# Group normalisation before a two-way scan: the fourth channel tile's scale made in one batch of four samples instead of three and one

## The reference, cut to what matters

```python
def step(prev, x_i):
    y = jnp.einsum('oc,nch->noh', Wc, prev) + conv_b[None, :, None]
    y = jnp.where(y >= 0, y, prelu_a * y)
    cur = y + x_i
    return (cur, cur)
# v = group norm of x (32 groups of 16 channels, over the group's channels, H and W)
_, fwd_rest = jax.lax.scan(step, x[0], x[1:])                  # over W, forwards
_, bwd_rest = jax.lax.scan(step, fl[-1], fl[:-1], reverse=True)  # and back
x = x + conv(group_norm(x))
```

## Time and profile before

| | |
|---|---|
| median of 3 runs | 378.11 us (378.09 to 378.15) |
| the profiled execution | 378.27 us, of which the span that the trace shows is 376.5 us |
| PE busy | 352.3 us, 94% of the span |
| DVE / ACT / POOL busy | 286.5 / 226.7 / 19.3 us |
| head: last x piece read to PE's first k = 3 unit | about 4 us, at 34.9 to 38.7 us |

### The profile page before, as it was taken

One profiled execution on the slowest core, in us unless ns is written; L12 is line 12 of the kernel. 1 busy time (PEld: TensorE's weight loads), 2 busy tenths in 40 slices (PEclk: granted clock), 3 DMA queues, 4 the chain that ended last, 5 costly groups with the idle time before them and its releaser, 6 DMA issues.

```text
span 376.5 us, 10089 instructions
## 1 busy us (share of the span) xinstructions
PE 352.3 (94%) x3102; PEld 350.7 (93%) x3102; DVE 286.5 (76%) x925; ACT 226.7 (60%) x798; POOL 19.3 (5%) x30
## 2 busy tenths in 40 slices
PE   0169999999999999999999999999999999999996
PEld 0169999999999999999999999999999999999996
DVE  2678897888888888656656778778787787787786
ACT  3764566566565565665655656656656556566564
POOL 2177100000000000000000000000000000000000
PEclk9999999999999999999999999999999999999999
DMA  8998000000000000000000112212212112122122
GB/s 313 419 415 303 3 0 0 1 0 0 1 0 0 0 1 0 0 0 0 0 0 0 58 61 78 84 56 84 84 56 84 73 66 84 58 81 84 56 111 84
DMA packets 10664, 26.30 MB, mean 70 GB/s; under 512 B 1312, under 2 KB 1568, under 8 KB 10656
## 3 DMA queue, kind: packets, MB, share of 16 engines
q1 hardware_dynamic: 10512, 26.22, 18.0%
q10 hardware_dynamic: 144, 0.00, 0.0%
HBM read 13.63 MB, written 12.58 MB: 70 GB/s over the span
## 4 chain that ended last, share of the span: by engine, by line
PE 90%; DMA 5%; SPq 2%; ACT 1%; DVE 1%; issue 1%; POOL 0%; DVEq 0%; ACTq 0%
PE psum L309 88%; DMA xin<-in_x 5%; SPq L217 2%; PE psum L263 1%; PE psum L273 1%; ACT above L368 0%; DVE state L398 0%; POOL rstd L539 0%; ACT state L331 0%; DVE state L445 0%; ACT state L334 0%; PE psum L256 0%; PE psum L243 0%; PE psum L251 0%; DVE state L440 0%
## 5 line engine op out<-in xcount | busy, mean ns | idle before, releaser
L309 PE MATMUL psum<-state,w_t 128*128 (+1 forms) x2976 | 332.9, 275 | 0.1
L309 PEld LDWEIGHTS psum<-state,w_t 128*128 128x128 f32 x2976 | 332.5, 192 | 0.4 <-DVE state L445 0.3
L368 ACT ACTIVATE above<-psum,params 128x128 f32<-128x128 f32 x376 | 139.8, 372 | 131.8 <-PE psum L309 128.9
L440 DVE TENSOR_TENSOR state<-above,state 128x128 f32 (+1 forms) x376 | 108.3, 288 | 67.1 <-ACT above L368 66.2
L370 ACT ACTIVATE below<-psum,negative 128x128 f32<-128x128 f32 x376 | 140.0, 372 | 0.0
L445 DVE SCALAR_TENSOR_TENSOR state<-below,negative,state 128x128 f32 (+1 forms) x376 | 123.3, 348 | 7.0 <-DVE state L440 0.2
L487 DVE TENSOR_TENSOR state<-state,xin (+1 forms) x45 | 30.8, 684 | 0.1
L380 DVE BATCH_NORM_STATS2 bstat<-xin 128x6 f32<-128x512 f32 x34 | 21.6, 676 | 11.9 <-DMA xin<-in_x 11.9
L398 DVE TENSOR_SCALAR state<-xin,mean,rstd 128x320 f32<-128x320 f32 (+2 forms) x72 | 28.1, 437 | 0.4 <-POOL rstd L539 0.4
L243 PE MATMUL psum<-chan,centre 128*128 128x64 f32 (+1 forms) x10 | 2.4, 328 | 18.0 <-DVE chan L394 18.0
L243 PEld LDWEIGHTS psum<-chan,centre 128*128 128x128 f32 x10 | 1.9, 240 | 18.1 <-issue 13.5
(11 more groups left out here) (27 smaller groups left out, 23.1 us busy)
## 6 DMA issues: line engine op xcount, KB each, us to landing
out_y<-state SPq DMA_DIRECT2D x47, 256.0 KB, 2.0
xin<-in_x SPq DMA_DIRECT2D x13, 768.0 KB, 12.8
xin<-in_x SPq DMA_DIRECT2D x5, 256.0 KB, 18.3
xin<-in_x SPq DMA_DIRECT2D x2, 512.0 KB, 19.4
w_t<-in_w SPq DMA_DIRECT2D x4, 256.0 KB, 11.2
out_y<-state SPq DMA_DIRECT2D x1, 192.0 KB, 1.9
out_y<-state SPq DMA_DIRECT2D x1, 64.0 KB, 1.6
params<-in_par ACTq DMA_DIRECT2D x1, 2.5 KB, 4.9
```

Source lines behind the costliest of these rows:

```text
L309: mm = nc.tensor.matmul(psum[:, 4 * par + o, 0:COLS], w_t[:, k, o * P:(o + 1) * P], xs[k], start=k == 0, stop=k == 3)
L368: nc.scalar.activation(above[:, par, o, :], z, ACT.Relu, bias=params[:, o:o + 1], scale=1.0).then_inc(above_done, 1)
L440: nc.vector.tensor_tensor(sts[o], above[:, par, o, :], sts[o], ALU.add).then_inc(part_done, 1)
```

## The change

Tile 3 becomes one batch of four samples (`LAST` = 3), its squares, variances and means are ACT's like those of the other tiles, and there is one `scale` for it. `OWN` goes from 3 to 1 and `AHEAD` from 2 to 4: DVE normalises w = 0 for the four samples, then w = 1 to 7 for the four samples, and then does step 0. On PE the lists of `FIRST` are two.

```diff
-FIRST = [[(0, 0)], [(0, 1)],
-         [(1, 0), (0, 2), (0, 3), (1, 1), (2, 0), (1, 2), (2, 1),
+FIRST = [[(0, 0)],
+         [(0, 1), (1, 0), (0, 2), (0, 3), (1, 1), (2, 0), (1, 2), (2, 1),
           (3, 0), (3, 1), (2, 2), (3, 2), (1, 3), (2, 3), (3, 3)]]
-BATCHES = [(0, 0, 4), (1, 0, 4), (2, 0, 4), (3, 0, 3), (3, 3, 4)]
+BATCHES = [(0, 0, 4), (1, 0, 4), (2, 0, 4), (3, 0, 4)]
-SPREAD = [16, 16, 16, 32, 64]
+SPREAD = [16, 16, 16, 32]
-OWN = 3
+OWN = 1
-AHEAD = 2
-PER_STEP = [3, 3, 3, 3, 2, 2, 2]
+AHEAD = 4
+PER_STEP = [3, 3, 3, 2, 2, 2, 2]
...
             group_sums(3)
             first_units(FIRST[0])
-            group_deviations(4)
             group_variances(3)
-            group_sums(4)
             first_units(FIRST[1])
-            group_variances(4)
-            first_units(FIRST[2])
...
-            channel_stats(b - 1).then_inc(chan_done, 1)
+            channel_stats(b - 1)
             unit_stats(b, 2).then_inc(stats_done, 1)
             channel_stats(b).then_inc(chan_done, 1)
...
-            dve.wait_ge(dev_done, LAST + 1)
-            nc.vector.tensor_scalar(dev2[:, k, n:N], gdev(LAST)[:, :, 0], gdev(LAST)[:, :, 0], None,
-                                    ALU.mult).then_inc(last_dev2_done, 1)
-            dve.wait_ge(gvar_done, LAST + 1)
-            nc.vector.tensor_scalar(var_eps[:, k, n:N], gvar(LAST)[:, :, 0], EPS, None,
-                                    ALU.add).then_inc(last_var_done, 1)
-            nc.vector.tensor_copy(mean[:, k, n:N], gmean(LAST)[:, :, 0]).then_inc(mean_kept, 1)
             dve.wait_ge(mean_kept, LAST + 1)
-            dve.wait_ge(rstd_done, LAST)
+            dve.wait_ge(rstd_done, LAST + 1)
             for m in range(n):
                 normalise(m, k, 0, OWN)
-            dve.wait_ge(rstd_done, LAST + 1)
             normalise(n, k, 0, OWN).then_inc(first_done, 1)
...
                     if (t, c) == (KT - 2, EARLY // CHUNK - 1):
-                        scale(LAST - 1)
                         scale(LAST)
```

More of the change, by code:

```diff
@@ L126, in scan_program @@
         dev2_done = sem("dev2_done")
-        last_dev2_done = sem("last_dev2_done")
         gvar_done = sem("gvar_done")
         var_done = sem("var_done")
-        last_var_done = sem("last_var_done")
         mean_kept = sem("mean_kept")
@@ L254, in group_variances @@
             def group_variances(t):
-                pe.wait_ge(*((last_dev2_done, 1) if t == LAST else (dev2_done, t + 1)))
+                pe.wait_ge(dev2_done, t + 1)
                 nc.tensor.matmul(gvar(t), same_group[:, :], spread_over(t, dev2),
@@ L359, in _ @@
             unit_stats(7)
-            group_values(3)
+            group_values(LAST)
             act.wait_ge(negated, 1)
@@ L537, in scale @@
                 k, n0, n1 = BATCHES[t]
-                pool.wait_ge(*((last_var_done, 1) if t == LAST else (var_done, t + 1)))
+                pool.wait_ge(var_done, t + 1)
                 nc.gpsimd.tensor_tensor(rstd[:, k, n0:n1], var_eps[:, k, n0:n1], minus_half[:, n0:n1],
```

## The result

The changed kernel is slower: 380.03 us median of 5 (379.94 to 380.27) against 378.15 of 5 in the same session, ratio 1.0049 (95% interval 1.0038 to 1.0060), +1.88 us. The forecast was +1.1; the direction was right, the time lies above the range.

A forecast was written before the change was run, and what follows sets the result against it. PE's back-to-back scan multiplies (332.9 of 376.5 us) were taken as the bound. PE's step 1 moving from 40.41 to 41.52 gave +1.1, a median of 379.2 us; range +0.8 to +1.4 with 70%.

The forecast's parts named there:

- The lead that the batch of three gave DVE: Before step 0: the batch of three let DVE run three normalisations ahead; without it DVE starts at 38.11, 0.79 later.
- The seven-row instructions: Four on DVE before step 0: following after 0.42, lasting 0.50, ending at 40.75, so PE's step 1 starts 1.11 later.
- the line through three and five rows: DVE normalisations: three rows follow after 0.28, five after 0.35, 1.0 ns per element, extended to seven rows.
- rival 2: Seven-row instructions are fast or hidden, ending by 40.2; only `first_done`'s delay counts: +0.5 to +0.6, 378.65; 15%.
- No loss in steps 1 to 3: DVE's step plus three ten-row instructions, 3.37, fits below PE's 3.58; nothing added, some 0.1 once if it fails.
- rival 4: PE's clock falls to 1.2 GHz in its idle gaps before step 1: some 2.3 lost, 381.5 with the rest; 3%.
- Four rows in place of twelve: DVE's one-row normalisations: each lasts 0.30, follows after 0.22; first four done at 39.07 against 38.54, PE's units +0.53.
- No cost or gain: Items put at nothing, among them POOL's last multiply: it ends near 39.0 and is wanted at 40.8.
- rival 3: POOL's last multiply blocks DVE's one-row instructions: `first_done` and all behind it 0.9 later, +2.0, 380.1; 8%.
- the wake-up: Before step 0's first addition: DVE's wait for its own last normalisation costs 0.04, so it starts at 40.79.
- both rules: Trainium skill on DVE: two-port mode needs outermost dimensions both even, or odd and equal; GpSimd and two-port instructions block each other.

The follow-up runs named there:

- a1: The changed kernel with POOL's last multiply put ahead of the power of tile 3 instead of behind it; 379.71 us.
- b1: The kernel before, its batches of three samples and one kept, with only the split into one row and seven taken over; 379.38 us.
- d2: The changed kernel with POOL's last multiply of four rows cut into two of two rows, back to back; 379.99 us.
- c4: The changed kernel with DVE's wait for `norm_done` moved from tile 0's first addition of step 0 to tile 3's; 379.89 us.
- c3: The kernel before with one row ahead, then three per sample, four rows behind steps 0 and 1, POOL's last multiply after `first_done`, moved waits; 377.81 us.
- c2: The changed kernel's batch of four in c3's order of rows, multiply and waits; 379.29 us.
- c1: The changed kernel with three rows ahead (`OWN` 3, `AHEAD` 2, old `PER_STEP`) and the batch's variances and means made by DVE, not ACT; 379.02 us.
- d1: The changed kernel with POOL's multiply ahead of the power, batch variances and means by DVE, and the `norm_done` wait at tile 3's first addition; 379.02 us.

## Why the prediction was wrong

*Right.* The lead that the batch of three gave DVE, and its loss: the power was due at 36.99 and came at 36.80, or 36.89 with the head's 0.09; it took 1.01 as the earlier trace rows had it; DVE started 0.69 later than before on the same clock, 0.79 was forecast. The seven-row instructions: pace 0.415, length 0.49 and 0.50, as the line through three and five rows gave it; rival 2 is out. That step 0's first addition would wait for them and not for ACT. No loss in steps 1 to 3. PE's clock stayed up: the granted clock is 1.00 from 36 to 42 us, and after the hole of 1.41 us the 14 multiplies again took 1.80; rival 4 is out.

*Wrong: the step "Four rows in place of twelve".* It took 0.30 for the first one-row instruction from the pace of three-row ones, and `first_done` at 39.07. The trace before had POOL's multiply on three- and five-row instructions only, which are of the other family, so their undisturbed pace said nothing about one row. Under "No cost or gain" the multiply was looked at only for the moment when its result is wanted, and put at nothing. Measured: 0.93, a hold of 0.64. This was rival 3, given 8% and priced at 0.9 as if DVE lost the whole multiply; it lost what was left of it after DVE's arrival at 37.92. That the rival's 380.1 lies next to the measured 380.03 is partly luck: its hold was 0.26 too long, and the 0.19 of the wake-up below was missing. The prediction had both rules before it and used the first only for the speed of seven rows, not for the mode of one.

*Wrong: the wake-up.* A wait for DVE's own result was priced at 0.04, as between two additions. It cost 0.23, in the changed kernel and in a1, b1 and d2 alike: 0.19 more. Several waits stand in front of this addition; which of them takes the time was not tried apart. In c4 the others still stand there without the one for `norm_done`, and the addition follows at DVE's own pace, so they cost nothing by themselves. c4 also shows what the wait and the end of the last instruction cost together, 0.31.

*Not foreseen, and hidden:* the hole behind the first normalisation. By a1 it would have cost 0.24 (0.45 in place of 0.21) had the hold not covered it.

*The sum on one clock.* Forecast start of PE's step 1: 41.52. With the hold (+0.64) and the wake-up (+0.19), less the earlier power (0.10) and a pace a little quicker (0.05 to 0.1), it is 42.15 to 42.20; measured 42.08 + 0.09 = 42.17. The 0.1 between these 1.76 and the median's 1.88 is of the size of the hiccups in the scan.

*A sum beside the forecast.* If the seven-row instructions were fast, they would end at 40.28 by the prediction's own rows, and with its 0.04 the first addition would be at 40.32: +0.64 and not the second rival's +0.57. Nothing else hangs on it.

*Open.* What makes the hiccups, which sit near 69, 100 and 133 us and cost 0.1 to 0.3 each (c3's profiled execution has none); in c2 and before it is DVE that starts late on data already there. Why DVE's second instruction comes late behind 2.9 us of idle time and not behind 0.4 to 1.3: c1 and d1 close the hole with two small instructions, but whether the idle time or the instructions count was not tried apart.

## What to carry to other kernels

Before a DVE instruction gets another shape, ask which mode the new shape runs in and what POOL does at that moment: here an even number of rows was faster alone and lost 0.64 to 0.73 us beside one POOL multiply of 1.04 us. Cutting a batch's count of instructions is worth nothing if the first batch is what lets the next engine start: let the early part run ahead of the last one. Work put under a cover must fit it as dispatched, and its completion should be waited for only where its result is read.

## What the runs showed of the hardware

- A held DVE instruction ended 0.04 to 0.05 us after POOL's (38.85 and 38.81; 38.93 and 38.88; 38.83 and 38.79; 38.59 and 38.55; in c4 38.95 and 38.91). POOL's multiply kept its 1.04 us, so only DVE paid.
- POOL's power of one value did not hold the one-row instructions that started beside it: 0.30 each at 37.38 and 37.59 in b1 (power 37.24 to 37.79), at 37.31 and 37.52 in c3 (37.17 to 37.72). No normalisation started beside a power of three or four values.
